# A decoder layer on one core: self-attention moved by most of a unit, both GELU halves together, and the eight PSUM banks dealt out anew

## What is computed

```python
x = x + self_attention(layernorm(x), wq, wk, wv, wo)              # 2 heads of 64, rotary, causal, softmax
x = x + cross_attention(layernorm(x), ctx, Wq, Wk, Wv, Wo, bq..)  # 16 heads of 8, 1601 keys, softmax
x = x + ffn(layernorm(x), W1, b1, W2, b2, scale)                  # hidden 512, exact GELU
# the ffn's weights are changed by the batch's own tokens: with lt = x[:, 1:17], even = lt[::2], odd = lt[1::2],
#   m1 = (even[:4, :, None] * odd[:4, None, :]).reshape(512, 128)   is added to W1, times scale
#   m2 = (even[4:, :, None] * odd[4:, None, :]).reshape(128, 512)   is added to W2, times scale
```

## Time and profile before

| | us |
|---|---|
| median of 3 runs (461.84 to 470.38) | 461.98 |
| profiled execution | 460.36 |
| its span, first to last instruction | 458.6 |
| PE busy (84%) | 385.6 |
| DVE busy (71%) | 327.4 |
| ACT busy (67%) | 305.7 |
| POOL busy (21%) | 94.1 |
| VectorE's maxima, 512 instructions | 257.8 |
| ScalarE's exponentials, 416 | 222.7 |

### The profile page before, as it was taken

How to read it: one execution, slowest core, us unless ns; L and a number is a source line. 1 busy time by engine, 2 the same in 40 slices (tenths; PEclk the granted TensorE clock), 3 DMA queues, 4 the chain that set the end, 5 groups by cost and what they waited for, 6 DMA issues and landing times.

```text
span 458.6 us, 9602 instructions
## 1 busy us (share of the span) xinstructions
PE 385.6 (84%) x3632; PEld 180.0 (39%) x3632; DVE 327.4 (71%) x777; ACT 305.7 (67%) x630; POOL 94.1 (21%) x107
## 2 busy tenths in 40 slices
PE   0855879999999889999788989999879999979606
PEld 0535112445443335444335444535335443324205
DVE  2551887978989988798687888797978989910100
ACT  1312014697878777978597778788896899897411
POOL 3530000513100043424000052560000042000050
PEclk9956555999999999999798999999998999997855
DMA  7053470303116220440160321521302310000010
GB/s 251 7 215 95 153 212 39 110 1 109 55 46 168 95 70 16 155 147 18 51 171 2 95 86 36 211 73 41 98 13 76 107 50 1 2 0 1 13 46 11
DMA packets 23387, 36.09 MB, mean 79 GB/s; under 512 B 1654, under 2 KB 20886, under 8 KB 23342
## 3 DMA queue, kind: packets, MB, share of 16 engines
q1 hardware_dynamic: 23342, 35.49, 24.7%
HBM read 19.68 MB, written 11.97 MB: 69 GB/s over the span
## 4 chain that ended last, share of the span: by engine, by line
PE 47%; DVE 27%; ACT 9%; DMA 6%; issue 5%; SPq 2%; POOL 2%; ACTq 0%; DVEq 0%; POOLq 0%
DVE part_max L580 19%; PE wsum L878 14%; PE score L892 10%; PE ring L909 7%; ACT probs L749 4%; PE ring L1039 3%; DMA q_rows<-q_parts 3%; PE ring L999 2%; PE ring L945 2%; PE ring L1031 2%; DMA q_unit<-consts 2%; DVE xn L616 1%; PE ring L934 1%; SPq L399 1%; ACT L749 1%
## 5 line engine op out<-in xcount | busy, mean ns | idle before, releaser
L580 DVE TENSOR_REDUCE part_max<-ring 128x1 f32<-128x401 f32 x512 | 257.8, 566 | 47.1 <-PE ring L909 46.6
L749 ACT ACTIVATE probs<-score 128x512 f32<-128x512 f32 (+1 forms) x416 | 222.7, 597 | 63.5 <-PE score L892 60.2
L909 PE MATMUL ring<-k_unit,q_unit 51*128 51x401 bf16 x512 | 150.0, 359 | 15.7 <-DMA q_unit<-consts 10.9
L878 PE MATMUL wsum<-probs,v_unit 128*32 128x256 f32 (+1 forms) x1664 | 137.0, 398 | 0.5 <-ACT unit_ctx L754 0.2
L892 PE MATMUL score<-q_unit,k_unit 51*128 51x256 bf16 (+1 forms) x832 | 125.2, 279 | 9.2 <-ACT probs L749 8.5
L892 PEld LDWEIGHTS score<-q_unit,k_unit 51*128 51x128 bf16 (+1 forms) x832 | 46.4, 97 | 104.9 <-ACT probs L749 61.6
L909 PEld LDWEIGHTS ring<-k_unit,q_unit 51*128 51x128 bf16 x512 | 47.8, 95 | 45.1 <-DVE part_max L580 27.3
L878 PEld LDWEIGHTS wsum<-probs,v_unit 128*32 128x32 f32 (+1 forms) x1664 | 34.8, 109 | 47.6 <-issue 27.4
L492 POOL TENSOR_TENSOR k_parts<-k_full,c_sb 128x802 bf16<-128x802 f32 x7 | 10.7, 1522 | 174.7 <-ACT k_full L791 174.7
L760 ACT ACTIVATE q_unit<-ring 3x512 bf16<-3x512 bf16 x32 | 18.6, 582 | 24.2 <-PE ring L920 23.9
L720 DVE TENSOR_TENSOR y_out<-ring,x_b 128x256 f32<-128x256 f32 x4 | 1.7, 425 | 35.9 <-PE ring L1039 35.9
(11 more groups left out here) (99 smaller groups left out, 330.2 us busy)
## 6 DMA issues: line engine op xcount, KB each, us to landing
k_unit<-k_rows SPq DMA_DIRECT2D x32, 300.2 KB
v_unit<-v_aug SPq DMA_DIRECT2D x16, 234.0 KB, 6.3
ctx_sb<-ctx_t SPq DMA_DIRECT2D x4, 800.5 KB, 8.9
k_rows<-k_parts SPq DMA_DIRECT2D x4, 601.5 KB, 4.6
k_rows<-k_parts SPq DMA_DIRECT2D x4, 599.2 KB, 3.7
even<-ffn_rows SPq DMA_DIRECT2D x4, 512.0 KB, 4.0
k_rows<-k_parts SPq DMA_DIRECT2D x4, 401.0 KB, 5.0
k_rows<-k_parts SPq DMA_DIRECT2D x4, 399.5 KB, 4.3
```

What stands on the lines that cost most here:

```text
L580: v_.tensor_reduce(part_max[:, par, q, head, hp, c:c + 1], ring[s][:, 0:CW], AX.X, ALU.max)\
L749: a_.activation(probs[0:rows, i % PB, :], score[i % EB][0:rows, :], ACT.Exp)\
L878: last = mm(wsum[32 * j:32 * j + 32, 0:S], v_unit[0:rows, u, VQ * t + VW * j:VQ * t + VW * j + 32], probs[0:rows, i % PB, S * (j // 2):S * ...
L909: mm(ring[s][:, 0:CW], q_unit[rows, u, hp, P * q:P * (q + 1)], k_unit[rows, u, L * hp + (CW - 1) * c:L * hp + (CW - 1) * c + CW], start=Tr ...
```

## The change

It has six parts.
1. Four score banks and a ring of three (`EB = 4`, `NR = 3`).
2. Weighted sums are made for two tiles at a time: at tiles 1, 3, 5, 7, 9 and 11, and a single one at 12 (`PV_AT`).
3. Self-attention of a batch starts in unit 3 of two batches before (`ln1`, `xT`, `qk`, `qks`) and goes on through units 0 and 1; keys and the query split are in unit 1, values in unit 2. Batch 1's first four steps stand in the start. `AHEAD` and `COUNT` deal the maxima out anew; 38 stand ahead of unit 0.
4. The probabilities are divided by the row sum on GpSimd (`pn`) before their turn; `av` then gives the transposed output directly, and `aT` is left out. The scores of both heads are made under `e1`, the heads alternating.
5. `h0` and `h1` stand together at tile 11 of unit 2, `out` in unit 3.
6. In the last batch the changed W1 and W2 come from products that broadcast one token to all partitions (`low0`, `low1`) and from VectorE, with no DMA and no GpSimd.

```diff
-EB = 3
+EB = 4
-NR = 4
+NR = 3
 SIDE = {
-    (0, 0): [("prep", "K0")], (0, 2): [("prep", "K1")], (0, 3): [("prep", "ln1")], (0, 5): [("prep", "xT")],
-    (0, 6): [("post", "OT")], (0, 7): [("prep", "qk")], (0, 8): [("prep", "qks"), ("post", "Wo")],
-    (0, 11): [("prep", "e0"), ("prep", "e1"), ("post", "ln3")], (0, 12): [("prep", "K2")],
-    (1, 0): [("prep", "soft")], (1, 1): [("post", "x3T"), ("prep", "K3")], (1, 2): [("prep", "v")],
-    (1, 3): [("prep", "pT0"), ("prep", "pT1")], (1, 4): [("prep", "store0")], (1, 5): [("prep", "av")],
-    (1, 7): [("prep", "aT")], (1, 9): [("prep", "wo")], (1, 10): [("post", "low")],
-    (1, 12): [("prep", "store1"), ("prep", "ln2")],
-    (2, 1): [("prep", "x2T")], (2, 3): [("prep", "q")], (2, 4): [("prep", "V0")], (2, 5): [("prep", "split")],
-    (2, 6): [("prep", "V1")], (2, 8): [("prep", "V2")], (2, 10): [("prep", "V3")], (2, 12): [("prep", "load")],
-    (3, 0): [("ctx", 2)], (3, 2): [("post", "h0")], (3, 5): [("post", "h1")], (3, 8): [("post", "out")],
+    (3, 0): [("ctx", 2)],
+    (3, 1): [("prep", "ln1", 2)], (3, 4): [("prep", "xT", 2)], (3, 5): [("post", "out", -1)],
+    (3, 7): [("prep", "qk", 2)], (3, 9): [("prep", "qks", 2)],
+    (0, 1): [("prep", "e0", 1), ("prep", "e1", 1)], (0, 4): [("prep", "soft", 1)], (0, 5): [("prep", "v", 1)],
+    (0, 6): [("prep", "pn", 1), ("post", "OT", -1)], (0, 8): [("post", "Wo", -1)],
+    (0, 9): [("prep", "pT0", 1), ("prep", "pT1", 1)], (0, 11): [("prep", "av", 1)], (0, 12): [("post", "ln3", -1)],
+    (1, 0): [("prep", "wo", 1)], (1, 1): [("post", "x3T", -1)], (1, 2): [("prep", "K0", 1)],
+    (1, 3): [("prep", "ln2", 1)], (1, 4): [("prep", "K1", 1)], (1, 5): [("prep", "x2T", 1)],
+    (1, 7): [("prep", "q", 1)], (1, 8): [("prep", "K2", 1)], (1, 9): [("prep", "K3", 1), ("prep", "split", 1)],
+    (1, 10): [("prep", "store0", 1)],
+    (2, 1): [("prep", "V0", 1)], (2, 2): [("prep", "store1", 1)], (2, 3): [("prep", "V1", 1)],
+    (2, 4): [("post", "low", -1)], (2, 5): [("prep", "V2", 1)], (2, 7): [("prep", "V3", 1)],
+    (2, 8): [("prep", "load", 1)], (2, 11): [("post", "h0", -1), ("post", "h1", -1)],
 }
-AHEAD = (8, 16, 8, 8)
-COUNT = ((3, 3, 2, 1, 2, 3, 2, 2, 1, 2, 1, 1, 1), (3, 3, 3, 2, 3, 2, 3, 3, 2, 2, 2, 2, 2),
-         (3, 2, 3, 2, 3, 1, 2, 3, 2, 3, 3, 3, 2), (3, 3, 3, 3, 3, 3, 3, 3, 3, 3, 3, 3, 4))
+AHEAD = (14, 14, 8, 9)
+AHEAD_FIRST = 6
+COUNT = ((2, 1, 3, 2, 2, 2, 2, 3, 2, 1, 2, 2, 2), (2, 3, 2, 2, 3, 3, 3, 3, 3, 2, 1, 3, 3),
+         (3, 3, 3, 3, 2, 3, 3, 3, 2, 2, 3, 3, 4), (3, 2, 3, 2, 3, 2, 3, 2, 3, 2, 2, 2, 3))
+COUNT_FIRST = (3, 2, 3, 3, 2, 3, 3, 3, 3, 2, 2, 3, 2)
+PV_AT = {1: (-2, -1), 3: (0, 1), 5: (2, 3), 7: (4, 5), 9: (6, 7), 11: (8, 9), 12: (10,)}
-START_PLAN = ([("prep", name, 0) for name in PREP_ALL] + [("ctx", 2, 1)] + [("M", 0, k) for k in range(MU)] +
-              [("mT", 0)] + [("M", 1, k) for k in range(AHEAD[1])])
+START_PLAN = ([("prep", name, 0) for name in PREP_FIRST] + [("ctx", 1)] +
+              [("prep", name, 1) for name in PREP_SECOND] + [("M", 0, k) for k in range(MU)] +
+              [("M", 1, k) for k in range(4)] + [("mT", 0)] + [("M", 1, k) for k in range(4, AHEAD_FIRST)])
...
+                    elif name == "pn":                                   # GpSimd
+                        pool.wait_ge(prsum_done, b + 1)
+                        for q in range(QT):
+                            cols = slice(0, P) if q == 0 else slice(P, 3 * P)
+                            for h in range(HA):
+                                last = g.tensor_scalar(prob_norm[:, h, cols], prob_self[:, h, cols],
+                                                       prob_rsum[:, q, h:h + 1], None, ALU.mult)
+                        last.then_inc(norm_done, 1)
...
-                elif name == "av":                                       # VectorE
+                elif name == "pn":
                     dve.wait_ge(soft_done, nb + 1)
                     v_.reciprocal(prob_rsum[:, :, :], prob_sum[:, :, :]).then_inc(prsum_done, 1)
-                    dve.wait_ge(prsum_done, nb + 1)
-                    s, n = take(item)
-                    v_.tensor_tensor(attn_out[:, :, :].rearrange("p q (h c) -> p (q h) c", h=HA),
-                                     ring[s][:, 0:S].rearrange("p (g c) -> p g c", c=DA),
-                                     prob_rsum[:, :, :].rearrange("p q h -> p (q h)").unsqueeze(2)
-                                     .to_broadcast([P, QT * HA, DA]), ALU.mult).then_inc(drained[s], 1)
...
+                elif name == "low0":                                     # VectorE; low1 likewise for W2
+                    v_.tensor_tensor(odd_scaled[:, :], xn3_t[:, 2:18:2], W("scale").to_broadcast([P, 8]), ALU.mult)
+                    for i in range(4):
+                        last = v_.scalar_tensor_tensor(
+                            out=w1_all[:, D * i:D * (i + 1)], in0=ring[s][:, D * i:D * (i + 1)],
+                            scalar=odd_scaled[:, i:i + 1], in1=W("W1")[:, D * i:D * (i + 1)],
+                            op0=ALU.mult, op1=ALU.add)
...
                 elif name == "av":                                       # TensorE
-                    for q in range(QT):
+                    for q, k in ((1, 0), (1, 1), (0, 0)):
                         for h in range(HA):
-                            for k in range(q + 1):
-                                last = mm(ring[s][:, D * q + DA * h:D * q + DA * (h + 1)],
-                                          prob_self_t[:, h, P * i:P * (i + 1)], v_self[:, k, DA * h:DA * (h + 1)],
-                                          start=k == 0, stop=k == q)
+                            last = mm(ring[s][DA * h:DA * (h + 1), P * q:P * (q + 1)],
+                                      v_self[:, k, DA * h:DA * (h + 1)],
+                                      prob_self_t[:, h, P * (q + k):P * (q + k + 1)], start=k == 0, stop=k == q)
-                elif name == "aT":
-                    turn_tokens(item, attn_out, ("av",))
+                elif name in ("low0", "low1"):
+                    for i in range(4):
+                        token = 2 * i + 8 * int(name[3]) + 1
+                        last = mm(ring[s][:, D * i:D * (i + 1)], C("ident")[:, token:token + 1].to_broadcast([P, P]),
+                                  xn3[:, 0, :], start=True, stop=True)
```

More of the change, by code:

```diff
@@ new lines @@
+    (1, 7): [("prep", "q", 1)], (1, 8): [("prep", "K2", 1)], (1, 9): [("prep", "K3", 1), ("prep", "split", 1)],
[3 more added lines that the diff above has]
+    (2, 8): [("prep", "load", 1)], (2, 11): [("post", "h0", -1), ("post", "h1", -1)],
+}
+PREP_FIRST = ["ln1", "xT", "qk", "qks", "K0", "K1", "e0", "e1", "K2", "K3", "store0", "soft", "pn", "v", "pT0", "pT1",
+              "av", "store1", "wo", "ln2", "x2T", "q", "split", "V0", "V1", "V2", "V3", "load"]
@@ L146, in max_head, with ahead @@
+def ahead(v):
+    return AHEAD_FIRST if v == 1 else AHEAD[v % UB]
 def max_head(k):
@@ L153, in unit_plan @@
     b, u = divmod(v, UB)
[L154 to L156 removed]
+    count = COUNT[u] if v else COUNT_FIRST
+    todo = [("M", v + 1, k) for k in range(ahead(v + 1), MU)] + [("M", v + 2, k) for k in range(ahead(v + 2))]
+    assert len(todo) == sum(count), (v, len(todo), sum(count))
     plan = []
     for t in range(KT):
[L159 removed]
+        now, todo = todo[:count[t]], todo[count[t]:]
         now = [item for item in now if item[1] < UNITS]
@@ L952, in prep @@
                     last.then_inc(filled[s], 1)
-                elif name in ("e0", "e1"):
+                elif name == "e1":
                     pe.wait_ge(qk_done, nb + 1)
-                    h = int(name[1])
-                    rows = slice(DA * h, DA * (h + 1))
-                    s = take(item)
+                    banks = [take(("prep", "e0", nb)), take(item)]
                     for q in range(QT):
-                        last = mm(ring[s][:, P * q:P * (2 * q + 1)], qk_rot[rows, P * q:P * (q + 1)],
-                                  qk_rot[rows, S:S + P * (q + 1)], start=True, stop=True)
-                    last.then_inc(filled[s], 1)
+                        for h in range(HA):
+                            rows = slice(DA * h, DA * (h + 1))
+                            last = mm(ring[banks[h]][:, P * q:P * (2 * q + 1)], qk_rot[rows, P * q:P * (q + 1)],
+                                      qk_rot[rows, S:S + P * (q + 1)], start=True, stop=True)
+                            if q == QT - 1:
+                                last.then_inc(filled[banks[h]], 1)
                 elif name in ("pT0", "pT1"):
-                    pe.wait_ge(soft_done, nb + 1)
+                    pe.wait_ge(norm_done, nb + 1)
                     s = take(item)
                     for i in range(3):
-                        last = turn(ring[s][:, P * i:P * (i + 1)], prob_self[:, int(name[2]), P * i:P * (i + 1)],
+                        last = turn(ring[s][:, P * i:P * (i + 1)], prob_norm[:, int(name[2]), P * i:P * (i + 1)],
```

(12 more changed lines are left out.)

70 lines of the change are left out of this document (43 added, 27 removed).

## The result

| | us |
|---|---|
| changed kernel, median of 4 runs (495.16 to 499.64) | 497.61 |
| before, median of 4 runs (461.84 to 470.38) | 462.28 |
| ratio, 95% interval | 1.074 (1.066 to 1.081) |
| profiled execution of the changed kernel, and its span | 497.86, 496.0 |

A median is over all runs of a round; a ratio leaves out the runs over 1.5% longer than the fastest of their kernel, so the two can differ a little.

A forecast was written before the change was run, and what follows sets the result against it. No single engine was taken to bound the kernel, though TensorE led in batch 2, VectorE close behind. Terms summed to -26.1 us: profiled 460.4 became 434.3, plus 1.6 for the median gave 436 us, range 424 to 453.

The forecast's parts named there:

- The middle: Units 1 to 3 and the batches: reduced engine work over an overlap share; +0.8, -10.0, -5.3 and -2.8 us.
- Rival (a): Units 1 to 3 and batches: VectorE and TensorE take turns waiting, batches 1 and 2 at 0.87; 448 us, chance 0.17.
- Pairs of weighted sums: Weighted sums of two tiles back to back: each pair saves TensorE 0.24 us, 1.4 us per unit.
- The banks: Ring of three: before the first score, a turn waits for the second bank to be drained, +1.0 us.
- rival (c): Side products next to pairs: VectorE idles 1.0 us more per place, 13 of 17 cases; 475 us, chance 0.06.
- Query split beside GpSimd: VectorE's query split, 1.4 us, meets GpSimd's key split and may double: +1.4 us.
- Keys: Units 1 and 2: key split to load landed 15.5 us, against 20 us to the first user; margin 4.5 us.
- rival (b): GpSimd's two key splits collide, next batch's first maxima wait about 4 us in three batches; 447 us, chance 0.09.
- unit 0: First unit: 24.2 us of TensorE work at density 0.94 gives 25.7 us, so -3.8 us.
- output product: Start: scaling probabilities on GpSimd and turns on the chain delay the attention's output product by 4.9 us.
- query stall of batch 1: Batch 1: TensorE's wait for the next batch's queries goes, as the split moves twelve tiles ahead of its first user.
- the tail: After the third norm, broadcast products replace the DRAM round trip, bringing the hidden product sooner: -6.0 us.

The follow-up runs named there:

- e3: Changed kernel with ring of four, three score banks and weighted sums tile by tile, rest as changed: 465.7 us, ratio 1.006.
- e5: Kernel before with the weighted sums in pairs, ring of four and three score banks kept: 476.6 us, ratio 1.039.
- e4: Kernel before with a ring of three and four score banks, nothing else: 482.9 us, ratio 1.042.
- e8: e3 with the first half of the keys stored ahead of the query split in SyncE's queue: 463.2 us, ratio 1.003.
- e9: e3 with the query split moved from tile 9 of unit 1 to tile 2 of unit 2, behind the second key store: 464.7 us, ratio 0.995.
- e7: Kernel before with the second GELU half directly behind the first, at tile 2 of unit 3: 451.9 us, ratio 0.981.
- e12: e9 with the first user of new keys and queries moved from tile 8 to tile 11 of unit 2: 455.0 us, ratio 0.981.

## Why the prediction was wrong

The terms of the sum against what they measured, and against the run with banks and pairs put back (e3), in us of the profiled executions:

| stage | forecast | changed kernel | e3 |
|---|---|---|---|
| to the end of the first unit | -2.8 | 0.0 | -3.3 |
| units 1 to 3 | +0.8 | +16.2 | +9.2 |
| batch 1 | -10.0 | +14.2 | +2.6 |
| batch 2 | -5.3 | +11.2 | +5.7 |
| batch 3 | -2.8 | +6.3 | +0.2 |
| tail | -6.0 | -10.5 | -9.1 |
| sum | -26.1 | +37.4 | +5.3 |

- **The middle: the step that failed.** It took TensorE's work down by the pairs and divided it by a round factor for the coupling of the engines (0.925 in units 1 to 3, 0.905 of two level engines in batches 1 and 2). In batch 2 TensorE was to be busy 80.1 of 88.5 us and was busy 90.1 of 105.0, a share of 0.86; in batch 1 and in units 1 to 3 the share is 0.86 too. Both parts of the step were wrong, the work and the overlap. Rival (a), 0.17, had the overlap right: the two engines take turns waiting, as unit 13 shows, and it put the busiest at 0.87. It too kept some 80 us of work a batch, and so came to 448.
- **Pairs of weighted sums.** The pair itself was sized right (1.00 us, score behind it 0.21); the sign of its effect was wrong. I booked 0.24 us per pair as a gain of TensorE. A pair keeps TensorE from both VectorE and ScalarE for 1.0 us, and of the 16.4 us that the sums gained in e5 the scores gave 10.0 back. In the kernel before the pairs alone cost 15 us.
- **The banks.** I saw the ring of three only in rival (c), with a price of 475 and a chance of 0.06, for one case (side products next to pairs). The argument against it was that TensorE leads in the stretches with a side product, so that VectorE's idling costs nothing. The runs of each alone in the kernel before show that the loss is largest just where side products stand (2.7 us in unit 9, 0.6 in unit 13, e4); TensorE's lead there did not cover it. And I took the fourth score bank for free cover; the last unit shows it to help only where pairs are (16.6 for 21.2 us, with single sums 17.5 for 16.8), and it is paid for with a ring bank that costs 20 us in the kernel before (e4). (c) named the right mechanism and priced it too low, 475 for 497.6: with a ring of three and pairs even unit 13, without side products, lost 3.5 us. Its 13 places of 17 also leave out the `post` items; by the plan, 16 of 23 places a batch have a side product with sums behind it.
- **Query split beside GpSimd.** Booked as +1.4 us of VectorE; measured +2.7 in the changed kernel and +4.8 in e8. The error was to count it as work. It is a stretch in which the ring isn't drained, so TensorE stops as well, and its clock falls behind it (0.54 in the stage after it in e8, 0.87 in the changed kernel, 1.00 before). Putting it elsewhere took 5.2 us off unit 1 (e9).
- **Keys.** The margin of 4.5 us rested on 12 tiles at 1.7 us and on landing times of a quieter stage. The store queued behind the query split, the loads took 7.8 us and not 2; in e3 TensorE waited 11.4 us for them in three batches. That is the price of rival (b), 0.09, about 4 us a batch, by another cause: GpSimd's second key split began 3.54 us after it was free, so the two did not run into each other; the order in SyncE's queue did it (e8).
- **One reading.** The sum for unit 0 divides by "today's density of 0.94"; the earlier trace rows has 28.60 of 29.50, 0.97, which gives -4.6 and not -3.8. It is small beside the rest.
- **Right:** start and first unit in sum, once banks and pairs are put back (-3.3 in e3 for -2.8); output product 4.5 later (4.9), partly by luck, since the turns (1.54 for 0.92) and the products (1.56 for 2.1) missed in opposite directions and the reciprocal came 1.1 earlier than in the kernel before (25.73 for 26.81), which was not foreseen; seven table loads besides the first; the query stall of batch 1 gone, though replaced; the six table loads less, 7.7 us of ScalarE, gave 9.6 in the kernel before (e7), with the block in unit 3. **Right in direction, small in size:** the tail, -10.5 for -6.0, because I kept the low clock for it.

## What to carry to other kernels

Where two consumers live off one producer through a few banks, ask how long the producer serves neither at a stretch, and not only how busy it is in total: here larger, cheaper blocks cost 15 us and a bank taken from one side for the other 20, each alone. Price such a change where side work stands too, since that is where each alone cost most. Read a cast or subtraction moved beside GpSimd as a hold on every bank that VectorE should drain (the maxima themselves kept their 567 ns). And of a change with six parts, try each alone: two of these gave 18 us by themselves, so the four others cost some 53 in all: 32 from banks and pairs, some 21 from the new placement with the scaling on GpSimd, by subtraction. Of those 21, moving the query split and its first user got back about 11 (e3 to e12, 2.5% by the ratios); the rest is open.

## What I had not expected of the hardware

VectorE's cast and subtraction of 128x256 took 1.50 and 1.88 us beside GpSimd's 1.6 and 1.7 us instructions and 0.29 and 0.43 alone: VectorE waited out the other's whole instruction. The same DRAM write of the query parts landed in 1.82, 4.25 and 6.54 us. The write of 6.54 was issued 1.1 us behind the issue of two key loads, the one of 4.25 3.3 us behind (the start of the kernel before), and the one of 1.82 9 us behind (the start of the changed kernel). But the write of the earlier trace rows took 3.61 with no key load issued in the 15 us before it, so the cause stays open.
